# A two-layer decoder on one NeuronCore: the second cross attention's scores from side-by-side key parts, and its output bias moved to GpSimd

## The reference

```python
def _L1_xattn_ref(q, k, mask, Wq, bq, Wk, bk, Wv, bv, Wo, bo):
    qh = jnp.einsum('bld,dh->blh', q, Wq) + bq
    kh = jnp.einsum('bld,dh->blh', k, Wk) + bk
    vh = jnp.einsum('blh,hv->blv', kh, Wv) + bv
    scores = jnp.einsum('bqh,bkh->bqk', qh, kh)
    scores = jnp.where(mask[:, None, :] == 0, jnp.float32(-10000.0), scores)
    probs = jax.nn.softmax(scores, axis=-1)
    out = jnp.einsum('bqk,bkh->bqh', probs, vh)
    return jnp.einsum('bqh,hv->bqv', out, Wo) + bo
```

## Time and profile before

| what | us |
|---|---|
| median of 3 runs (lowest, highest) | 3655.15 (3652.3, 3658.6) |
| span of the profiled execution | 3652.9 |
| PE busy over the span | 3377.2 (92%) |
| DVE busy | 2631.2 (72%) |
| ACT busy | 2280.8 (62%) |
| POOL busy | 1022.4 (28%) |

### The profile page before, as it was taken

One profiled execution on the slowest core, in us unless ns is written; L12 is line 12 of the kernel. 1 busy time (PEld: TensorE's weight loads), 2 busy tenths in 40 slices (PEclk: granted clock), 3 DMA queues, 4 the chain that ended last, 5 costly groups with the idle time before them and its releaser, 6 DMA issues.

```text
span 3652.9 us, 60630 instructions
## 1 busy us (share of the span) xinstructions
PE 3377.2 (92%) x21090; PEld 2546.5 (70%) x21090; DVE 2631.2 (72%) x7153; ACT 2280.8 (62%) x4067; POOL 1022.4 (28%) x1576
## 2 busy tenths in 40 slices
PE   5999999999999948999999999999999876999998
PEld 4677777777777636777777777777777555766664
DVE  5588888888888754667777777777777543788876
ACT  3677777777777632456555555665555543677776
POOL 2144444443444431222222222222222210000000
PEclk8999999999999979999999999999999877999999
DMA  7644545544454121444444444444444412011010
GB/s 192 100 91 87 85 88 95 99 83 83 96 105 78 24 87 34 75 82 93 93 88 89 89 93 91 90 92 88 90 93 87 73 29 76 12 35 35 24 35 24
DMA packets 203407, 283.34 MB, mean 78 GB/s; under 512 B 48929, under 2 KB 131874, under 8 KB 194274
## 3 DMA queue, kind: packets, MB, share of 16 engines
q1 hardware_dynamic: 203106, 279.46, 38.1%
HBM read 179.49 MB, written 96.73 MB: 76 GB/s over the span
## 4 chain that ended last, share of the span: by engine, by line
PE 74%; ACT 9%; DVE 7%; DMA 4%; issue 3%; POOL 1%; SPq 1%; PEld 0%; POOLq 0%; ACTq 0%; PEldq 0%; DVEq 0%
PE ps L827 35%; PE ps L976 9%; PE ps L1000 9%; PE ps L1014 6%; PE ps L1198 5%; ACT q_stack L1666 4%; PE ps L951 3%; DMA qk_scratch<-parts 2%; PE ps L980 2%; ACT pt L1683 1%; PE ps L1074 1%; PE ps L1025 1%; DMA k_stack<-qk_scratch 1%; PE ps L886 1%; PE ps L1084 1%
## 5 line engine op out<-in xcount | busy, mean ns | idle before, releaser
L1683 ACT ACTIVATE pt<-ps 128x512 f32<-128x512 f32 x1280 | 734.2, 597 | 370.5 <-PE ps L1000 359.9
L976 PE MATMUL ps<-k_stack,q_stack 96*128 96x512 f32 (+3 forms) x2048 | 596.0, 355 | 41.9 <-ACT q_stack L1666 10.7
L1886 POOL TENSOR_SCALAR_AFFINE_SELECT pt<-pt 128x256 f32<-128x256 f32 x1024 | 392.1, 419 | 714.7 <-ACT pt L1683 714.7
L1355 DVE CUSTOM_DVE_ANT_0 ps<-ps,future 128x512 f32<-128x512 f32 (+3 forms) x1024 | 481.5, 515 | 142.9 <-PE ps L976 140.4
L1000 PE MATMUL ps<-q_stack,k_stack 100*128 100x512 f32 (+3 forms) x2048 | 539.5, 345 | 26.3 <-ACT q_stack L1666 22.1
L976 PEld LDWEIGHTS ps<-k_stack,q_stack 96*128 96x128 f32 x2048 | 383.8, 196 | 96.3 <-ACT q_stack L1666 16.9
L1000 PEld LDWEIGHTS ps<-q_stack,k_stack 100*128 100x128 f32 x2048 | 352.2, 195 | 120.0 <-ACT q_stack L1666 36.2
L1348 DVE TENSOR_REDUCE nmax<-ps 128x1 f32<-128x512 f32 (+2 forms) x768 | 358.0, 502 | 102.1 <-PE ps L980 99.9
L1892 POOL TENSOR_TENSOR rs<-rs 128x4 f32<-128x4 f32 x96 | 97.1, 1011 | 1066.6 <-DVE rs L1391 1066.6
L1666 ACT ACTIVATE q_stack<-ps 4x512 fp32r<-4x512 f32 x512 | 300.8, 587 | 65.0 <-PE ps L989 56.8
L1014 PE MATMUL ps<-pt,v_ones 128*32 128x512 f32 (+3 forms) x4096 | 311.4, 446 | 4.9 <-POOL pt L1886 4.9
(11 more groups left out here) (278 smaller groups left out, 7915.8 us busy)
## 6 DMA issues: line engine op xcount, KB each, us to landing
qk_scratch<-parts SPq DMA_DIRECT2D x64, 1024.0 KB, 5.5
q_stack<-qk_scratch SPq DMA_DIRECT2D x384, 128.0 KB, 4.9
k_stack<-qk_scratch SPq DMA_DIRECT2D x384, 128.0 KB, 5.6
gate_of<-gate_scratch SPq DMA_DIRECT2D x128, 256.0 KB, 5.5
x_mid<-x_ring SPq DMA_DIRECT2D x32, 512.0 KB, 3.6
x_ring<-x_mid SPq DMA_DIRECT2D x32, 512.0 KB, 5.9
x_ring<-in_x SPq DMA_DIRECT2D x16, 512.0 KB, 3.9
out_dram<-x_ring SPq DMA_DIRECT2D x16, 512.0 KB, 2.9
```

The source lines that it names most:

```text
L976: done = e.matmul(bank(bank_of[piece])[:, at:at + width], a.q[0:96, base + h, t * P:(t + 1) * P], a.k[0:96, base + h, 0:width], start=True ...
L1355: done = e.tensor_tensor_reduce(src, src, future[:, SEQ - width:SEQ], -1.0, 3e38, ALU.add, ALU.min, nmax[:, g % 2, to:to + 1])
L1683: e.activation(dst, src, ACT.Exp).then_inc(exp_up.sem)
L1886: done = e.affine_select(out=blk, in_=blk, compare_op=ALU.is_ge, fill=0.0, base=0, pattern=[[0, 2], [1, P]], channel_multiplier=-1)
```

## The change

The folded keys' high and low parts are put side by side in one array, `a_parts`. The scores of a token tile are now four matmuls and not six: the high part of x by both key parts (128 moving columns), the low part of x by the high key part (64 columns), for each half of the 256 channels. That leaves two halves in PSUM; DVE copies one to `sx3` and adds the other to it. The bias row is no longer added per batch: in the prologue DVE multiplies it by `seen` and adds it to `unseen`, which is then called `offset`. The output bias `co_b` is spread over 128 partitions by its transfer and added to x by POOL in a new piece `tb x1`; the product with a row of ones goes.

```diff
@@ the table: gpsimd, stage 3, and the list of pieces
+            "tb x1": [-26.6],
...
         put("tc", "x1", b)
+        put("tb", "x1", b)
@@ buffers
-        co_b, f2_b = sb(st3, "co_b_row", [1, DIM]), sb(st3, "f2_b_cols", [P, CT])
-        ones = sb(st3, "ones", [1, P])
+        co_b, f2_b = sb(st3, "co_b_rows", [P, DIM]), sb(st3, "f2_b_cols", [P, CT])
...
-        a_h, a_l = (sb(st3, f"a_{part}", [P, CT, keys_all], F32R) for part in "hl")
+        a_parts = sb(st3, "a_parts", [P, CT, BATCH, 2, CTX], F32R)
...
-        LN_BIAS = {"x0": xo_b, "a1": proj_b}
+        LN_BIAS = {"x0": xo_b, "a1": proj_b, "x1": co_b}
@@ PE, "cw"
-                    ops.append((ones[:, :], co_b[:, :]))
@@ PE, "cs"
-                        ops = []
-                        for c in range(CT):
-                            ops += three(ch[:, c, rows], cl[:, c, rows], a_h[:, c, keys], a_l[:, c, keys])
-                        done = product(e, bank(bank_of[piece])[:, t * CTX:(t + 1) * CTX], ops)
+                        both = bank(bank_of[piece])[:, 2 * t * CTX:2 * (t + 1) * CTX]
+                        done = None
+                        for c, part in ((0, ch), (0, cl), (1, cl), (1, ch)):
+                            wide = part is ch
+                            done = e.matmul(both if wide else both[:, 0:CTX], part[:, c, rows],
+                                            a_parts[:, c, b, :, :].rearrange("p a k -> p (a k)") if wide else a_parts[:, c, b, 0, :],
+                                            start=wide and c == 0, stop=wide and c == 1)
@@ DVE, end of the prologue
+                        for n in range(2):
+                            cols = slice(n * 512, n * 512 + 512)
+                            e.wait_ge(bq_up, n + 1)
+                            e.wait_ge(keys_lo, 12)
+                            e.tensor_tensor(tile32[:, n, :], bank(4 + n), seen[:, cols], ALU.mult).then_inc(mine.up())
+                            e.wait_ge(*mine.now)
+                            e.tensor_tensor(offset[:, cols], offset[:, cols], tile32[:, n, :], ALU.add).then_inc(mine.up())
@@ DVE, "cs"
-                    e.tensor_tensor(sc3[:, :, :], bank(bank_of[piece])[:, 0:TT * CTX].rearrange("p (t k) -> p t k", t=TT),
-                                    key_row(q_bias), ALU.add).then_inc(cs_add.sem)
+                    halves = bank(bank_of[piece]).rearrange("p (t a k) -> p t a k", t=TT, a=2)
+                    e.tensor_copy(sx3[:, :, :], halves[:, :, 1, :]).then_inc(mine.up())
+                    e.wait_ge(*mine.now)
+                    e.tensor_tensor(sc3[:, :, :], halves[:, :, 0, :], sx3[:, :, :], ALU.add).then_inc(cs_add.sem)
...
-                    e.tensor_tensor(sc3[:, :, :], sc3[:, :, :], key_row(unseen), ALU.add).then_inc(mine.up())
+                    e.tensor_tensor(sc3[:, :, :], sc3[:, :, :], key_row(offset), ALU.add).then_inc(mine.up())
@@ ACT, prologue
-                        for n in range(2):
-                            e.wait_ge(bq_up, n + 1)
-                            e.activation(q_bias[:, n * 512:n * 512 + 512], bank(4 + n), ACT.Copy)
@@ POOL, prologue
-                elif kind == "prologue":
-                    e.memset(ones[:, :], 1.0)
@@ SP, prologue
-                        e.dma_start(co_b[:, :], dram["co_b"].partition_broadcast(1)).then_inc(mask_in3, 16)
+                        e.dma_start(co_b[:, :], dram["co_b"].partition_broadcast(P)).then_inc(mask_in3, 16)
```

More of the change, by code:

```diff
@@ L741, in decoder @@
         cq_b, ck_b, cv_b = (sb(st3, f"{n}_cols", [P, CT]) for n in ("cq_b", "ck_b", "cv_b"))
-        co_b, f2_b = sb(st3, "co_b_row", [1, DIM]), sb(st3, "f2_b_cols", [P, CT])
-        ones = sb(st3, "ones", [1, P])
+        co_b, f2_b = sb(st3, "co_b_rows", [P, DIM]), sb(st3, "f2_b_cols", [P, CT])
         wf2 = sb(st3, "w_down", [P, FT, DIM])
         ff_c, fc = sb(st3, "ff_c", [P, 4 * FT]), sb(st3, "fc", [P, 12, FT])
-        a_h, a_l = (sb(st3, f"a_{part}", [P, CT, keys_all], F32R) for part in "hl")
+        a_parts = sb(st3, "a_parts", [P, CT, BATCH, 2, CTX], F32R)
         v_h, v_l = (sb(st3, f"v_{part}", [P, CT, BATCH, 2, CTX], F32R) for part in "hl")
-        q_bias, seen, unseen = (sb(st3, n, [P, keys_all]) for n in ("q_bias", "seen", "unseen"))
+        seen, offset = (sb(st3, n, [P, keys_all]) for n in ("seen", "offset"))
         W3 = Weights(st3, 3)
@@ L759, in decoder @@
         ch, cl = sb(st3, "xh3", [P, CT, SEQ], F32R), sb(st3, "xl3", [P, CT, SEQ], F32R)
-        sc3 = sb(st3, "sc3", [P, TT, CTX])
+        sc3, sx3 = sb(st3, "sc3", [P, TT, CTX]), sb(st3, "sx3", [P, TT, CTX])
         sm3 = sb(st3, "sm3", [P, 3, TT, 1])
@@ L1254, in vector @@
                         e.wait_ge(*mine.now)
-                        e.tensor_scalar(unseen[:, :], seen[:, :], 10000.0, -10000.0, ALU.mult, ALU.add)
+                        e.tensor_scalar(offset[:, :], seen[:, :], 10000.0, -10000.0, ALU.mult, ALU.add)
                         e.tensor_copy(bq[:, :, :], cq_b[:, :].unsqueeze(2).broadcast_to([P, CT, P])).then_inc(circle_up)
@@ L1628, in scalar @@
                                 done.then_inc(keys_hi)
-                            else:
-                                e.activation((k_h3, None, a_h)[q // 4][:, mt, cols], tile32[:, q % 2, :],
+                            elif q // 4 == 0:
+                                e.activation(k_h3[:, mt, cols], tile32[:, q % 2, :], ACT.Copy).then_inc(keys_hi)
+                            else:
+                                e.activation(a_parts[:, mt, n * 8:n * 8 + 8, 0, :],
+                                             tile32[:, q % 2, :].rearrange("p (b k) -> p b k", k=CTX),
                                              ACT.Copy).then_inc(keys_hi)
-                        for n in range(2):
-                            e.wait_ge(bq_up, n + 1)
-                            e.activation(q_bias[:, n * 512:n * 512 + 512], bank(4 + n), ACT.Copy)
                         for at, res in enumerate((sin_c, cos_c)):
```

10 lines of the change are left out of this document (6 added, 4 removed).

## The result

The changed kernel takes 3646.51 us (median of 7 runs, 3642.42 to 3649.08), the kernel before, run beside it, 3656.04 us (3652.3 to 3661.4). The ratio is 0.9972, with a 95% interval of 0.9961 to 0.9982: 9.5 us less by the medians, where 11.3 less was forecast. The interval leaves out 1, so the change is faster, if by little.

What follows compares the result with a forecast made beforehand. PE was taken to bound the steady part, busy 33.00 of 33.00 us. Prologue and first batches +5.3 and thirteen steady batches -16.6 gave -11.3, so 3655.15 us became 3643.9, rounded 3644, range 3634 to 3659.

Steps and rivals of the forecast that it cites:

- The likeliest case: Whole kernel: the terms come out as summed, 3639 to 3649 us; chance 0.48.
- `cs` on PE: Score product: 16 matmuls instead of 24 at 0.111 us each, saving 0.89 us per batch.
- `cw` on PE: Bias product, two passes of a one-row float32 matmul, disappears from PE: 0.74 us saved per steady batch.
- The copy and `bk`: DVE's added PSUM copy costs 0.46 us and delays the hand-over to `bk`: PE stalls 0.30 us per period.
- `fa` 6: Steady batch: `fb` 3 frees the bank just in time for `fa` 6's first matmul; 0.05 us allowed.
- `tb` in the steady part: POOL's addition starts 0.35 us after DVE's last earlier operation with two SBUF inputs; priced at nothing, a near thing.
- The holds in batches 0 and 1: DVE's shift waits behind POOL's `tb`, taking 2.4 us: 2.2 more, twice, +4.4 us.
- The clock that follows: Longer idle gaps may drop PE's clock over the start of batch 2: 0 to 3 us, taken as 1.5.
- The rival, that the shift is in first: Batches 0 and 1: DVE's shift starts before POOL's add reads, so no hold; 3638 us, chance 0.17.
- The prologue: DVE's two multiplies and two adds for the offset lie on the path at the prologue's end: +2.75 us.
- The first batches: `cs` 0 to 2 save 1.7, 1.25 and 0.9 us; DVE's copy, bare three times, costs 1.4.
- The thirteenth batch: Steady part: `cs` 3 to 15 and `cw` 3 to 15 counted as 13 x -1.28 = -16.6 us.

Runs made afterwards that it cites:

- the scores alone: Kernel after with the bias taken back to a product of `cw` and `tb x1` left out: ratio 0.9967 to the kernel before, median 3646.26 us.
- the all-narrow kernel: Kernel after with the eight 128-column matmuls of `cs` cut to 64 columns, leaving out one product: 3643.47 us, one run, no ratio.
- the bias alone: Kernel before with the bias added by POOL in `tb x1` and its product gone, scores unchanged: 3652.61 us, ratio 0.9985 to the kernel before.
- the shorter and the longer chain: Kernel after with DVE's copy and add made one reduction, 0.9956 to the kernel before; in another, the copy done twice, 0.9992.
- the kernel with one reduction: Kernel after with DVE's copy and add replaced by one reduction straight from PSUM: 3640.95 us, ratio 0.9956 to the kernel before.
- `tb` behind the shift: Kernel after with POOL's `tb x1` also waiting for DVE's shift of the batch before: 3637.51 us, ratio 0.9947 to the kernel before.
- the eight kernels: The kernels whose prologue is that of the kernel after: 70.92 to 72.63 us from DVE's last shift of stage 2 to `cs` 0, middle 71.7.
- the kernel with the offset later: Kernel after with DVE's four offset operations moved behind the point where all engines meet after the prologue: 3644.89 us, ratio 0.9963 to the kernel before.
- the one with the early `tb`: Kernel after with PE's `tc x1` put before `fd` 4, so POOL's `tb x1` starts earlier: 3667.19 us, ratio 1.0024 to the kernel before.

## Why the prediction was right, step by step

The likeliest case came true: 3646.5 us for 3644 forecast, inside that case's own 3639 to 3649. The mechanism was right in the steady part and at the two holds; that the sum fits as well as it does is luck in part, as the end of the list says. Of its steps:

- **`cs` on PE.** -0.89 forecast, 2.60 - 1.74 = -0.86 measured. Shown by the scores alone; that the columns don't count, by the all-narrow kernel; that the weights do is argued.
- **`cw` on PE.** -0.74 forecast, -0.76 in the period of the bias alone.
- **The copy and `bk`.** 0.46 was right to the hundredth; the stall was forecast as 0.30 and is 0.24, since the wider last matmul cost next to nothing. Shown by the shorter and the longer chain.
- **`fa` 6: the term that was mis-sized.** "It just holds ... I allow 0.05": it doesn't hold, and costs 0.17. I had `fb` 3 end 0.11 before PE wants the bank, and left out the way between them. In the kernel after `fb` 3 ends at 3437.75 + 0.74 = 3438.49 and `fa` 6 starts at 3438.64, 0.15 later; the kernel with one reduction has the same 0.15. And a product that starts late starts slowly: its second matmul is 0.31 behind the first, not 0.23. With 0.17 for 0.05 and 0.24 for 0.30 the period would have come out at 31.74; it is 31.77.
- **`tb` in the steady part.** Nothing forecast, nothing found; its lead is 0.48, 0.35 had been worked out. The prediction called it a near thing: 1.7 us more haste on PE's side makes it 1.70 per batch, somewhat under the 2.4 given for it.
- **The holds in batches 0 and 1.** 2.2 each forecast, 2.14 each measured. The hold is shown by the rows and by `tb` behind the shift. The clock that follows was put at 1.5 (0 to 3). It is 2.7 between the profiled executions of the kernel after and of that one, and next to nothing between all narrow and that one, so its size, and that the holds cause it, stay open. The rival, that the shift is in first, is out: it came 0.06 late.
- **The prologue.** 2.75 forecast, 3.1 by moving the operations away. Before to after the stretch grew by 0.8 only; with the middle of the eight kernels it is 1.5, where 1.85 was forecast. The 0.3 for the longer transfer was not tested by itself.
- **The first batches.** Their scores gained more than summed: `cs` 0 to 3 is 4.1 us shorter with the scores alone, where `cs` 0 to 2 and three copies had been put at -2.45. Part of that can be the clock, 0.92 in that execution and 0.88 before. The sum also forgot the bias products of `cw` 1 and 2, which lie in this stretch; without any hold it is 72.64 with the bias products of `cw` 1 to 3 and 71.61 without them.
- **The thirteenth batch.** Only twelve periods lie between `cs` 3 and `cs` 15. Behind `cs` 15 there are scores but no `cw`: 0.6 gained, and with the bias alone nothing (101.24 us for 101.21). The thirteenth `cw` is number 3, ahead of `cs` 3.

So the sum came within 1 us of the 12.3 because its errors went both ways: up to `cs` 3 the kernel did 2 us better than summed (+2.6 for +4.6), from there on 1 us worse (-14.9 for -15.9). The first of these is no firmer than one execution of each kernel: the all-narrow kernel, with the same holds, has 2.6 us less there (76.02 for 78.61).

## What to carry to other kernels

An idle gap ahead of an operation says that it has time to start, not that what hangs behind it has time to end: follow the chain from it to the next engine that waits, and count each hand-over (0.15 us here), before a cost is put at nothing. An operation on POOL that adds two SBUF tensors is free only where DVE has no operation with two SBUF inputs to start during it, however small; a wait that puts it behind the critical one cost nothing here and brought 7 us in the profile, 4.3 of them the holds. And where PE's clock changes level, one execution of each kernel can't price an edit: 2.7 us came and went there in kernels whose edits hardly touch the stretch.

## What the runs showed of the hardware

- DVE's operation on 4 columns with two SBUF inputs took 2.30 us behind the start of a POOL addition of two SBUF tensors, and 0.16 otherwise; one on 512 columns 2.73 for 0.69. One that had started 0.48 before POOL's kept its 0.69, and POOL's took 2.44 beside it, 2.34 in batches 0 and 1. Those with PSUM as an input (L1566, L1338) kept their length inside it. The Trainium skill ("SBUF — State Buffer", section "Who interferes with whom") has a DVE instruction with two SBUF inputs contend with a GpSimd one that reads SBUF, and whoever issues first keep the shared ports for the whole instruction. In the kernel after and in the one with the early `tb`, each such DVE operation that starts inside POOL's two-input addition ends with it or up to 0.55 behind it, which agrees.
- With one input POOL's row is longer, 2.78 to 2.81 us in 14 of 16 (2.92 and 3.03 in the others), and holds DVE for less, 0.74 and 0.84. By that rule of the Trainium skill L1560 would have ended behind 3417.74; it ended at 3416.52. The measurement stands; the reason is open.
- A DVE reduction that adds pairs of elements 64 apart in PSUM runs at the usual rate: 0.69 for 128x512.
- Matmuls of 128 and 64 columns stood 0.109 us from start to start where all had their own 128x128 weights, and 0.106 where all had 64 columns.
- After 3.76 us without work PE's next eight matmuls took 1.97 us, at a granted clock of 0.50, the lower of its two levels (1.2 GHz), and 1.09 after 1.62 us, at 1.00 (2.4 GHz). The idle time alone does not decide it: in the kernel with the offset later the same 3.76 us were followed by 1.52, and 3.98 us one batch on by 1.25.

```profile
3100.55 1.52 PE L952 MATMUL ps<-ident,x_ring 128*128 128x128 f32 x8 [3.76 <-ACT x_ring L1724]
3124.17 1.25 PE L952 MATMUL ps<-ident,x_ring 128*128 128x128 f32 x8 [3.98 <-ACT x_ring L1724]
```
